# Decoder layer, attention stage: the projections of the next batch spread over all four head steps, the output projection ahead of the transposes

## The chip, the cores and the metric

The kernel runs on one core of a Trainium2 chip. A core has five engines that run on their own and wait for each other through semaphores: TensorE (PE: matmuls and transposes, results into PSUM; its weight loads are listed apart as PEld), VectorE (DVE), ScalarE (ACT), GpSimd (POOL) and SyncE (SP, which here only issues DMAs). PSUM has eight banks of 128 x 512 fp32. The metric is the device time of one execution in microseconds (us).

## The reference

A decoder layer on x of 4 batches x 512 positions x 512 features: x plus attention of its layer norm, then a small cross attention, then a mixture of experts. The change touches the attention alone:

```
q = rope((x @ Wq.T).reshape(B, L, 32, 64))
k = rope((x @ Wk.T).reshape(B, L, 8, 64))
v = (x @ Wv.T).reshape(B, L, 8, 64)
attn = where(causal, q @ k.T * 64 ** -0.5, -inf)      # 4 query heads share a k/v head
out  = (softmax(attn) @ v) @ Wo.T
```

## The kernel before

The attention is worked in 8 groups (one k/v head and its 4 query heads), each group over 4 batches, each batch over 4 heads: 128 **head steps**. The functions `pe_group`, `act_group`, `dve_group` and `pool_group` write out, for each engine, one group's 16 head steps in a fixed order; nothing else sets the order. The first and the last group are written out; the six between run in a hardware loop `Fori` of two passes with three groups in its body (L634, L667, L709, L738; SP's at L607). In a step, c = 4b + h, b being the batch and h the head in it (0 to 3; this text says first to fourth step). Three heads are in work at once: scores and softmax of head n+1, the transposes of the probabilities of head n-1, and PV of head n-2.

All products are made in fp32r from a high and a low part ("hi" is a rounded copy made by ACT, "lo" the rest, made by DVE or POOL), so a projection is 12 matmuls (4 chunks of the features x 3 combinations). One step's parts, by function and line of before:

- `pe_scores` (L197): 8 matmuls into S_BANK. `dve_masked` (L411, at L421) scales and masks them into `probs` and takes the row's extreme; `act_exp` (L307) follows, `dve_recip` (L426), and POOL's `pool_norm` (L540) multiplies with it.
- `pe_ptrans` (L211, at L217): ten 128 x 128 transposes of `probs` in three units: unit 0 (four, T_BANK[0]), unit 1 (four, T_BANK[1]), unit 2 (two, T_BANK[0] again, issued at the start of the next step). `act_pt` makes pt_hi from the bank (L349), `dve_pt` pt_lo (L464, at L409). Unit 0 of the next head waits until unit 2's pt_lo is made, since they share a bank.
- `pe_pv` (L221, at L234): 8 matmuls; `act_opart` (L356) copies one half of the result, `dve_oadd` (L469, at L474) adds the other half into `o_f`. After two heads `act_o` makes o_hi and `dve_o` o_lo.
- `pe_wo` (L237, at L246): output projection of 128 positions, 6 matmuls into WO_BANK, one per step, for the batch before. `dve_woacc` (L480, at L484) adds it to `x_res`. The group's weights for it are split in batch 1: hi by `act_w2` at the end of the second step, lo by `dve_w2` in the third step, where `pe_wo` first waits for them (w2_lo_done).
- `pe_proj` (L179, at L184): one projection of the **next** batch into PJ_BANK. Index r = 2 is k and v together, r = 0 and 1 two heads of q each. `dve_rope_in` (L430) reads the bank, `pool_rope` (L533) and `act_rope` (L315) go on; `dve_q_lo` (L442) makes q's low part for two heads.
- `pe_vt` (L189, at L194): four small transposes of v into PJ_BANK, then `act_v` and `dve_v` read them.

In before, the first three steps of a batch hold one whole projection each (k/v, q of heads 0 and 1, q of heads 2 and 3), the fourth v's transposes. The first output tile of a batch is projected in the third step.

## Time and profile before

| | us |
|---|---|
| timed runs | 1640.63, 1640.20, 1631.22 (median 1640.2) |
| the profiled execution: its own time | 1635.06 |
| its span, first to last instruction | 1633.3 |
| PE busy | 1483.1 (91%) |
| DVE busy | 1372.1 (84%) |
| ACT busy | 1057.7 (65%) |
| POOL busy | 849.6 (52%) |

How to read it: the busy shares are averages over three stages. The layer norms and the first projections take about the first 55 us, the attention groups last until about 1050 us, the rest is cross attention and experts, which the change leaves alone. In a timeline a row is a start, a length, the engine, the line and operation, what it writes and reads, and in brackets the idle time before it and what ended that. Matmuls overlap, so the cost of one is the distance between starts and not its length.

### The profile page before, as it was taken

The page shows a single profiled execution, that of the slowest core. Times are in us where ns is not written, and L with a number is a line of the kernel's source. Part 1 is how long each engine was busy: PE and PEld are TensorE (multiplying, and loading weights), DVE is VectorE, ACT ScalarE, POOL GpSimd, SP SyncE. Part 2 cuts the span into 40 slices and gives each one's busy share as a digit, 9 for nine tenths or more (in the row PEclk, how much of TensorE's full clock was granted, in tenths as well). Part 3 has the DMA queues.
Part 4 walks back from the last instruction along what each step waited for, and adds up shares of the span by engine and source line. Part 5 has one row for each costly group of instructions (what it writes and reads, how often), then busy time and mean ns, then how long its engine had stood idle before and what let it go on. Part 6 is the DMA issues. An engine that isn't in the chain of part 4 may idle for free. (4 is left out here: it accounts for less than half of the span.)

```text
span 1633.3 us, 31312 instructions
## 1 busy us (share of the span) xinstructions
PE 1483.1 (91%) x8951; PEld 1306.6 (80%) x8951; DVE 1372.1 (84%) x3565; ACT 1057.7 (65%) x2464; POOL 849.6 (52%) x1033
## 2 busy tenths in 40 slices
PE   5789999999999899999999999688599999999994
PEld 4678888888888788878878877577489999999993
DVE  7789888898898788988988988577579988998892
ACT  3677777777777677777777777332166666666661
POOL 6667657657657557657657655267612233222321
PEclk9899999999999999999999999967599999999997
DMA  4000000000000000000000000112468778887765
GB/s 175 1 14 20 1 14 21 1 14 21 1 14 20 3 14 21 2 14 21 1 14 1 1 1 1 41 65 92 164 184 243 226 217 220 240 228 219 198 172 135
DMA packets 62032, 124.97 MB, mean 77 GB/s; under 512 B 20942, under 2 KB 21070, under 8 KB 61792
## 3 DMA queue, kind: packets, MB, share of 16 engines
q1 hardware_dynamic: 51408, 102.24, 19.6%
q0 software_dynamic: 10304, 20.59, 6.6%
q8 instruction: 77, 1.26, 0.3%
q14 instruction: 99, 0.81, 0.2%
q10 hardware_dynamic: 144, 0.07, 0.0%
HBM read 106.08 MB, written 24.71 MB: 80 GB/s over the span
## 5 line engine op out<-in xcount | busy, mean ns | idle before, releaser
L312 ACT ACTIVATE probs<-probs,neg_max 128x512 f32<-128x512 f32 (+3 forms) x512 | 281.7, 552 | 46.5 <-DVE neg_max L421 44.2
L545 POOL TENSOR_SCALAR probs<-probs,row_inv 128x512 f32<-128x512 f32 (+3 forms) x512 | 264.3, 535 | 44.4 <-DVE row_inv L428 44.4
L536 POOL TENSOR_TENSOR rot<-rot,sin 128x512 f32<-128x512 f32 (+1 forms) x96 | 123.6, 1288 | 303.4 <-DVE rot L440 299.1
L217 PE MATMUL bank<-ident,probs 128*128 128x128 f32 x1280 | 184.5, 275 | 59.6 <-DVE pt_lo L409 50.1
L409 DVE TENSOR_TENSOR pt_lo<-bank,pt_hi 128x512 fp32r<-128x512 f32 (+1 forms) x384 | 216.3, 591 | 25.8 <-ACT pt_hi L305 25.7
L305 ACT ACTIVATE pt_hi<-bank 128x512 fp32r<-128x512 f32 (+1 forms) x384 | 186.3, 518 | 71.6 <-PE bank L217 63.6
L421 DVE CUSTOM_DVE_ANT_0 probs<-bank,causal 128x512 f32<-128x512 f32 (+3 forms) x512 | 219.7, 482 | 10.1 <-issue 3.6
L1221 POOL DMA_INDIRECT acc<-ctx_raw,idx x46 | 74.5, 1619 | 294.9 <-ACT ctx_raw L1374 280.8
L217 PEld LDWEIGHTS bank<-ident,probs 128*128 128x128 f32 x1280 | 149.9, 140 | 94.9 <-DVE pt_lo L409 54.9
L1302 PE MATMUL bank<-xt_hi,gu_hi 128*128 128x256 f32 x736 | 208.4, 283 | 2.0 <-DVE xt_lo L409 1.5
L1302 PE MATMUL bank<-xt_lo,gu_hi 128*128 128x256 f32 x736 | 206.7, 281 | 0.0
L1302 PE MATMUL bank<-xt_hi,gu_lo 128*128 128x256 f32 x736 | 206.5, 281 | 0.0
L207 PE MATMUL bank<-k_hi,q_st 128*128 128x256 f32 (+2 forms) x512 | 172.3, 347 | 3.2 <-DVE xn_lo L409 3.2
L234 PE MATMUL bank<-pt_hi,v_st 128*128 128x256 f32 (+2 forms) x512 | 171.4, 346 | 1.6 <-DVE pt_lo L409 1.6
L207 PE MATMUL bank<-k_lo,q_st 128*128 128x256 f32 (+2 forms) x512 | 156.9, 328 | 0.0
L234 PE MATMUL bank<-pt_lo,v_st 128*128 128x256 f32 (+2 forms) x512 | 155.8, 326 | 0.0
L184 PE MATMUL bank<-xn_hi,w_hi 128*128 128x512 f32 x384 | 153.2, 399 | 0.4 <-DVE rot L440 0.4
L184 PE MATMUL bank<-xn_lo,w_hi 128*128 128x512 f32 x384 | 151.9, 396 | 0.0
L184 PE MATMUL bank<-xn_hi,w_lo 128*128 128x512 f32 x384 | 151.5, 395 | 0.0
L1302 PEld LDWEIGHTS bank<-xt_hi,gu_hi 128*128 128x128 f32 x736 | 139.2, 189 | 6.2 <-issue 2.8
L1302 PEld LDWEIGHTS bank<-xt_lo,gu_hi 128*128 128x128 f32 x736 | 139.5, 189 | 2.8
L1302 PEld LDWEIGHTS bank<-xt_hi,gu_lo 128*128 128x128 f32 x736 | 139.1, 189 | 0.0
(196 smaller groups left out, 3912.8 us busy)
## 6 DMA issues: line engine op xcount, KB each, us to landing
gu_raw<-in_gate_up SPq DMA_DIRECT2D x92, 512.0 KB, 4.2
dn_raw<-in_down SPq DMA_DIRECT2D x92, 256.0 KB, 3.8
w_raw<-in_wqkv SPq DMA_DIRECT2D x8, 768.0 KB, 4.1
w_raw<-in_wo_rows SPq DMA_DIRECT2D x8, 512.0 KB, 3.5
h_rows<-ln_h SPq DMA_DIRECT2D x16, 256.0 KB, 2.0
acc<-x_res SPq DMA_DIRECT2D x4, 1024.0 KB, 4.7
x_res<-in_x SPq DMA_DIRECT2D x3, 1024.0 KB, 11.4
ctx_raw<-in_ctx SPq DMA_DIRECT2D x2, 512.0 KB, 6.7
```

Of the source, the lines that this page charges most:

```text
L184: last = nc.tensor.matmul(PJ_BANK[:, :], w1[sp][:, c, r * P:(r + 1) * P], xn[mp][:, c, b * L:(b + 1) * L], start=first, stop=(c == DC - 1 ...
L207: last = nc.tensor.matmul(S_BANK[k][:, at:at + cols], q_st[:, h, i * P:(i + 1) * P], kk[:, kb, 0:cols], start=(a == 0), stop=(a == 1))
L217: last = nc.tensor.transpose(T_BANK[u % 2][:, k * P:(k + 1) * P], probs[:, hb, P_AT[i] + j * P:P_AT[i] + (j + 1) * P], ident[:, :])
L234: last = nc.tensor.matmul(dst, v_st[:, vb, j, :], rhs, start=(j == 0 and a == 0), stop=(j == QB - 1 and a == 1))
L305: nc.scalar.activation(dst, src, ACT.Copy).then_inc(sem_, 1)
L312: nc.scalar.activation(row, row, ACT.Exp, bias=neg_max[:, hb, i:i + 1], scale=-1.0, accum_out=row_sum[:, hb, i:i + 1]).then_inc(s["exp_don ...
L409: nc.vector.tensor_tensor(dst, src, hi.bitcast(F32), ALU.subtract).then_inc(sem_, 1)
L421: nc.vector.tensor_tensor_reduce(out=probs[:, hb, P_AT[i]:P_AT[i] + (i + 1) * P], in0=S_BANK[k][:, at:at + (i + 1) * P], in1=causal[:, (QB ...
L536: nc.gpsimd.tensor_tensor(rot[0:rows, :], rot[0:rows, :], sin[0:rows, :], ALU.mult).then_inc(s["rot_sin"], 1)
L545: nc.gpsimd.tensor_scalar(row, row, row_inv[:, hb, i:i + 1], 0.0, ALU.mult, ALU.add).then_inc(s["pnorm_done"], 1)
L1221: nc.gpsimd.indirect_dma_start(out=acc, out_offset=bass.IndirectOffsetOnAxis(ap=idx[:, 2 * tau + h:2 * tau + h + 1], axis=0), in_=y[:, 2 * ...
L1302: last = nc.tensor.matmul(GU_BANK[u % 3][:, side * TILE:(side + 1) * TILE], gu[sp_][:, ib, c, side, :], xts[mp][:, k, c, :], start=first, ...
```

## The change

- The twelve matmuls of a projection are cut into two pieces in different steps, and each of the four steps gets nine: the fourth step the first 9 of k/v (for the batch after the next), the first step the other 3 and, behind PV, the first 6 of q for heads 0 and 1, the second step the other 6 and, behind PV, the first 3 of q for heads 2 and 3, the third step the other 9.
- v's transposes stand at the fourth step's start and write T_BANK[1] in place of PJ_BANK, so they wait for the second pt_lo of the head before; the transposes of unit 1 wait for v_lo in that step.
- The output projection stands ahead of the eight transposes in every step (before: only in the first step). On DVE, adding it to x_res stands ahead of o_f.
- ACT's and DVE's work on the second pair of q heads moves from the next batch's first step to the fourth step; v's from the fourth step's end to its start.
- The group loops are written out on all engines, SP among them.

```
+KV_FIRST, Q01_FIRST, Q23_FIRST = 9, 6, 3
...
+        def pe_proj(pe, b, r, begin=0, end=3 * DC):
+            for n in range(begin, end):
+                c, (sp, mp) = n // 3, PASSES[n % 3]
+                last = nc.tensor.matmul(PJ_BANK[:, :], w1[sp][:, c, r * P:(r + 1) * P], xn[mp][:, c, b * L:(b + 1) * L],
+                                        start=(n == 0), stop=(n == 3 * DC - 1))
+            if end == 3 * DC:
+                last.then_inc(s["proj_done"], 1)
...
+        def pe_vt(pe, m, heads_before):
             pe.wait_ge(s["vt_done"], m + 1)
             settled(pe)
+            wait(pe, s["pt_lo_done"], heads_before and 3 * heads_before - 1)
             for j in range(QB):
-                last = nc.tensor.transpose(PJ_BANK[:, j * HD:(j + 1) * HD], v_t[:, j * P:(j + 1) * P], ident[HD:P, HD:P])
+                last = nc.tensor.transpose(T_BANK[1][:, j * HD:(j + 1) * HD], v_t[:, j * P:(j + 1) * P], ident[HD:P, HD:P])
...
+            if u == 1 and n % G == 2 and n < HEADS * GROUPS - G:
+                pe.wait_ge(s["v_lo_done"], n // G + 2)
...
                 if d_begun:
                     pe_ptrans(pe, dn_ - 1, (r + d - 1) % 3, 2)
+                if h == 3 and next_batch:
+                    pe_vt(pe, m + 1, dn_)
                 if more:
                     pe_scores(pe, n + 1, m if h < G - 1 else m + 1, (h + 1) % G, (b + (h == G - 1)) % 2)
...
                 if h == 0 and next_batch:
-                    pe.wait_ge(s["v_lo_done"], m + 1)
-                    pe_proj(pe, (b + 1) % B, 2)
+                    pe_proj(pe, (b + 1) % B, 2, KV_FIRST)
                 if h == 1 and next_batch:
...
+                    pe_proj(pe, (b + 1) % B, 0, Q01_FIRST)
                 if h == 2 and next_batch:
...
+                    pe_proj(pe, (b + 1) % B, 1, Q23_FIRST)
+                if h == 3 and batch_after:
+                    if b == 2:
+                        pe.wait_ge(s["w1_lo_done"], 3 * g + 4)
                     pe.wait_ge(s["rope_in"], 3 * m + 6)
-                    pe_vt(pe, m + 1)
+                    pe_proj(pe, (b + 2) % B, 2, 0, KV_FIRST)
                 if dh == 3 and d_last:
                     pe_wo(pe, dm - 1, (db - 1) % 2, 2)
-                if d_here:
-                    pe_ptrans(pe, dn_, (r + d) % 3, 0)
-                    pe_ptrans(pe, dn_, (r + d) % 3, 1)
-                if d_begun:
-                    pe_pv(pe, dn_ - 1, dm if dh else dm - 1, (d + 1) % 2, (db if dh else db + 1) % 2)
                 if dh in (1, 2) and d_last:
                     if dh == 1 and db == 1:
                         pe.wait_ge(s["w2_lo_done"], 2 * g + 2)
                     pe_wo(pe, dm - 1, (db - 1) % 2, dh - 1)
                 if dh == 0 and d_before_last:
                     pe_wo(pe, dm - 2, db % 2, 3)
+                if d_here:
+                    pe_ptrans(pe, dn_, (r + d) % 3, 0)
+                    pe_ptrans(pe, dn_, (r + d) % 3, 1)
+                if d_begun:
+                    pe_pv(pe, dn_ - 1, dm if dh else dm - 1, (d + 1) % 2, (db if dh else db + 1) % 2)
+                if h == 0 and next_batch:
...
+                    pe.wait_ge(s["rope_in"], 3 * m + 4)
+                    pe.wait_ge(s["vt_done"], m + 2)
+                    pe_proj(pe, (b + 1) % B, 0, 0, Q01_FIRST)
+                if h == 1 and next_batch:
...
+                    pe.wait_ge(s["rope_in"], 3 * m + 5)
+                    pe_proj(pe, (b + 1) % B, 1, 0, Q23_FIRST)
...
-                if h == 0 and begun and front:
-                    act_rope(act, m, 2, b % 2)
-                if h in (1, 2) and next_batch:
+                if h == 3 and next_batch:
+                    act_v(act, m + 1, (b + 1) % 2)
+                if h and next_batch:
                     act_rope(act, m + 1, h - 1, (b + 1) % 2)
...
-                if h == 0 and begun and front:
-                    dve_q_lo(dve, m, 2, b % 2)
-                if h == 2 and next_batch:
-                    dve_q_lo(dve, m + 1, 1, (b + 1) % 2)
+                if h == 3 and next_batch:
+                    dve_v(dve, m + 1, (b + 1) % 2)
+                if h >= 2 and next_batch:
+                    dve_q_lo(dve, m + 1, h - 1, (b + 1) % 2)
...
-                with pe.Fori(0, (GROUPS - 2) // 3) as q:
-                    for i in range(1, 4):
-                        pe_group(pe, 3 * q + i, i % 3)
+                for g in range(1, GROUPS - 1):
+                    pe_group(pe, g, g % 3)
```

PE, third step of batch 1 in the last group: `w_hi`/`w_lo` with `o_hi`/`o_lo` is the output projection, `probs` the transposes, `v_st` PV. Before, from the second unit of transposes:

```order
L217 MATMUL bank<-ident,probs 128x128 [waits pt_lo_done]
L217 MATMUL bank<-ident,probs 128x128 x3
L234 MATMUL bank<-pt_hi,v_st 128x512 [waits oadd_done,v_lo_done,pt_lo_done]
L234 MATMUL bank<-pt_lo,v_st 128x512
L234 MATMUL bank<-pt_hi,v_st 128x384
L234 MATMUL bank<-pt_lo,v_st 128x384
L234 MATMUL bank<-pt_hi,v_st 128x256
L234 MATMUL bank<-pt_lo,v_st 128x256
L234 MATMUL bank<-pt_hi,v_st 128x256
L234 MATMUL bank<-pt_lo,v_st 128x256
L246 MATMUL bank<-w_hi,o_hi 128x512 [waits wo_out_done,o_lo_done,w2_lo_done]
L246 MATMUL bank<-w_lo,o_hi 128x512
```

Of the change, at the same place, from the last two projection matmuls (`xn`):

```order
L186 MATMUL bank<-xn_lo,w_hi 128x512
L186 MATMUL bank<-xn_hi,w_lo 128x512
L251 MATMUL bank<-w_hi,o_hi 128x512 [waits wo_out_done,o_lo_done,w2_lo_done]
L251 MATMUL bank<-w_lo,o_hi 128x512
L251 MATMUL bank<-w_hi,o_lo 128x512
L251 MATMUL bank<-w_hi,o_hi 128x512
L251 MATMUL bank<-w_lo,o_hi 128x512
L251 MATMUL bank<-w_hi,o_lo 128x512
L222 MATMUL bank<-ident,probs 128x128 [waits pt_lo_done,pnorm_done]
L222 MATMUL bank<-ident,probs 128x128 x3
```

The output projection with its wait for w2_lo_done has moved from behind PV to ahead of the transposes.

PE, fourth step that follows it: the last two matmuls of the scores (`k_lo`, `k_hi`), v's transposes (`v_and_o`), the eight transposes of the probabilities. Before:

```order
L207 MATMUL bank<-k_hi,q_st 128x256
L207 MATMUL bank<-k_lo,q_st 128x256
L194 MATMUL bank<-ident,v_and_o 128x64 [waits rope_in,vt_done]
L194 MATMUL bank<-ident,v_and_o 128x64 x3
L217 MATMUL bank<-ident,probs 128x128 [waits pt_lo_done,pnorm_done]
L217 MATMUL bank<-ident,probs 128x128 x3
```

Of the change, from the start of that step:

```order
L222 MATMUL bank<-ident,probs 128x128 [waits pt_lo_done]
L222 MATMUL bank<-ident,probs 128x128
L197 MATMUL bank<-ident,v_and_o 128x64 [waits vt_done,pt_lo_done]
L197 MATMUL bank<-ident,v_and_o 128x64 x3
L210 MATMUL bank<-k_hi,q_st 128x512 [waits masked_done,q_lo_done,k_lo_done]
```

v's transposes now stand ahead of the scores and wait for a pt_lo; between the scores and the eight transposes stand nine projection matmuls and the output projection (rows like those shown above).

DVE, the same fourth step in the first group, from pt_lo of unit 2 on: `q_st` is q's low part, `x_res` the sum with the output projection, `o_f` the sum of PV's halves. Before:

```order
L409 TENSOR_TENSOR pt_lo<-bank,pt_hi 128x256 [waits pt_hi_done]
L428 RECIPROCAL row_inv<-row_sum 128x4 [waits exp_done]
L409 TENSOR_TENSOR pt_lo<-bank,pt_hi 128x512 [waits pt_hi_done] x2
L409 TENSOR_TENSOR v_st<-bank,v_st 128x4x64 [waits v_hi_done]
L474 TENSOR_TENSOR o_f<-bank,v_and_o 64x512 [waits o_lo_done,opart_done]
L484 TENSOR_TENSOR x_res<-bank,x_res 128x512 [waits wo_done]
```

Of the change:

```order
L422 TENSOR_TENSOR pt_lo<-bank,pt_hi 128x256 [waits pt_hi_done]
L422 TENSOR_TENSOR v_st<-bank,v_st 128x4x64 [waits v_hi_done]
L459 TENSOR_TENSOR q_st<-rope,q_st 64x512 [waits rope_hi]
L460 TENSOR_TENSOR q_st<-rope,q_st 64x512
L441 RECIPROCAL row_inv<-row_sum 128x4 [waits exp_done]
L422 TENSOR_TENSOR pt_lo<-bank,pt_hi 128x512 [waits pt_hi_done] x2
L497 TENSOR_TENSOR x_res<-bank,x_res 128x512 [waits wo_done]
L487 TENSOR_TENSOR o_f<-bank,v_and_o 64x512 [waits o_lo_done,opart_done]
```

v's low part and two instructions for q now stand ahead of the reciprocal and of the two pt_lo; o_f stands last.

## Rows read from the trace of the kernel before

**Rows 1.** Windows: busy us (and instructions) of each engine in one group.
```profile
319.58:442.60 123.02, 117.18 (x674) 101.44 (x673) 109.89 (x291) 94.08 (x237) 78.15 (x100) 1.00 0.04 12
```

**Rows 2.** Waits in the attention: engine, who ended them, us, times, longest.
```profile
PE bank L217 <- DVE pt_lo L409: 46.2, 47, 2.6
```

**Rows 3.** Timeline of PE: a second step, then the third step's start and output projection.
```profile
332.56 0.38 PE L217 MATMUL bank<-ident,probs 128*128 128x128 f32 x2
...
334.08 0.40 PE L184 MATMUL bank<-xn_hi,w_hi 128*128 128x512 f32 x1
...
336.82 1.03 PE L217 MATMUL bank<-ident,probs 128*128 128x128 f32 x8
337.61 0.48 PE L234 MATMUL bank<-pt_hi,v_st 128*128 128x512 f32 x1
...
338.99 0.40 PE L246 MATMUL bank<-w_hi,o_hi 128*128 128x512 f32 x1
...
340.38 0.38 PE L217 MATMUL bank<-ident,probs 128*128 128x128 f32 x2
...
347.04 0.50 PE L246 MATMUL bank<-w_hi,o_hi 128*128 128x512 f32 x1
```

**Rows 4.** Timeline of PE: v's transposes in a fourth step and what follows.
```profile
319.58 0.46 PE L194 MATMUL bank<-ident,v_and_o 64*128 64x64 f32 x4
321.19 1.09 PE L217 MATMUL bank<-ident,probs 128*128 128x128 f32 x8 [1.15 <-DVE pt_lo L409]
```

**Rows 5.** Timeline of PE: v's transposes, first and last of 31 such rows.
```profile
74.28 0.46 PE L194 MATMUL bank<-ident,v_and_o 64*128 64x64 f32 x4
...
1001.95 0.46 PE L194 MATMUL bank<-ident,v_and_o 64*128 64x64 f32 x4
```

**Rows 6.** Waits in the attention that nothing in the profile explains: ACT.
```profile
ACT pt_hi L305 <- issue: 5.1, 1, 5.1
```

**Rows 7.** Timeline of ACT and DVE behind the PV of rows 3.
```profile
339.19 0.59 ACT L305 ACTIVATE v_and_o<-bank 64x512 f32<-64x512 f32 x1 [0.51 <-PE bank L234]
...
339.82 0.68 DVE L474 TENSOR_TENSOR o_f<-bank,v_and_o 64x512 f32<-64x512 f32 x1 [0.21 <-ACT v_and_o L305]
340.58 0.69 DVE L484 TENSOR_TENSOR x_res<-bank,x_res 128x512 f32<-128x512 f32 x1
```

**Rows 8.** Timeline of DVE: the third step of batch 1, masking to pt_lo.
```profile
341.37 0.69 DVE L421 CUSTOM_DVE_ANT_0 probs<-bank,causal 128x512 f32<-128x512 f32 x1
...
343.02 0.42 DVE L409 TENSOR_TENSOR pt_lo<-bank,pt_hi 128x256 fp32r<-128x256 f32 x1
343.36 0.80 DVE L409 TENSOR_TENSOR o_lo<-o_f,o_hi 128x512 fp32r<-128x512 f32 x1
...
345.61 1.29 DVE L409 TENSOR_TENSOR w_lo<-w_raw,w_hi 128x512 fp32r<-128x512 f32 x2
...
348.13 1.26 DVE L409 TENSOR_TENSOR pt_lo<-bank,pt_hi 128x512 fp32r<-128x512 f32 x2
```

**Rows 9.** Timeline of ACT at the same place.
```profile
340.53 0.63 ACT L305 ACTIVATE o_hi<-o_f 128x512 fp32r<-128x512 f32 x1 [0.75 <-DVE o_f L474]
341.07 1.14 ACT L305 ACTIVATE w_hi<-w_raw 128x512 fp32r<-128x512 f32 x2
342.24 0.39 ACT L305 ACTIVATE pt_hi<-bank 128x256 fp32r<-128x256 f32 x1
```

**Rows 10.** Windows as in rows 1; behind POOL stands the granted clock.
```profile
1018.00:1021.00 3.00, 3.00 (x12) 2.71 (x12) 1.41 (x3) 1.09 (x3) 2.05 (x4) 0.50 0.00 0
...
135.00:137.70 2.70, 0.99 (x9) 0.72 (x7) 2.59 (x11) 1.45 (x5) 2.70 (x5) 1.00 0.00 0
```

**Rows 11.** Timeline of PE: a step of the last batch.
```profile
1017.00 1.41 PE L217 MATMUL bank<-ident,probs 128*128 128x128 f32 x8 [2.13 <-DVE pt_lo L409]
```

**Rows 12.** Timeline of DVE in a first step, and of POOL beside rows 8.
```profile
327.77 0.68 DVE L409 TENSOR_TENSOR o_lo<-o_f,o_hi 128x512 fp32r<-128x512 f32 x1
...
341.57 2.06 POOL L545 TENSOR_SCALAR probs<-probs,row_inv 128x512 f32<-128x512 f32 x4
```

More of the change, by code:

```diff
@@ L177, in pe_ln @@
             last.then_inc(s["lnt_done"], 1)
-        def pe_proj(pe, b, r):
-            first = True
-            for c in range(DC):
-                for sp, mp in PASSES:
-                    last = nc.tensor.matmul(PJ_BANK[:, :], w1[sp][:, c, r * P:(r + 1) * P], xn[mp][:, c, b * L:(b + 1) * L],
-                                            start=first, stop=(c == DC - 1 and (sp, mp) == PASSES[-1]))
-                    first = False
-            last.then_inc(s["proj_done"], 1)
-        def pe_vt(pe, m):
+        def pe_proj(pe, b, r, begin=0, end=3 * DC):
[6 more added lines that the diff above has]
+        def pe_vt(pe, m, heads_before):
             pe.wait_ge(s["vt_done"], m + 1)
             settled(pe)
+            wait(pe, s["pt_lo_done"], heads_before and 3 * heads_before - 1)
             for j in range(QB):
-                last = nc.tensor.transpose(PJ_BANK[:, j * HD:(j + 1) * HD], v_t[:, j * P:(j + 1) * P], ident[HD:P, HD:P])
+                last = nc.tensor.transpose(T_BANK[1][:, j * HD:(j + 1) * HD], v_t[:, j * P:(j + 1) * P], ident[HD:P, HD:P])
             last.then_inc(s["v_tr"], 1)
@@ L395, in act_group @@
                     act_pt(act, dn_, d % 2, 1)
-                if h == 3 and next_batch:
-                    act_v(act, m + 1, (b + 1) % 2)
                 if d_begun:
@@ L522, in dve_group @@
                     dve_woacc(dve, dm - 1, (db - 1) % B, 2)
-                if h == 3 and next_batch:
-                    dve_v(dve, m + 1, (b + 1) % 2)
-                if d_begun:
-                    dve_oadd(dve, dn_ - 1, (d - 1) % 2, HEADS // 2 * g + (d - 1) // 2)
                 if dh in (1, 2) and d_last:
@@ L606, in _ @@
                 sp_w2(sp, 0)
-                with sp.Fori(1, GROUPS) as g:
+                for g in range(1, GROUPS):
                     sp_w1(sp, g)
@@ L666, in _ @@
                 act_group(act, 0, 0)
-                with act.Fori(0, (GROUPS - 2) // 3) as q:
-                    for i in range(1, 4):
-                        act_group(act, 3 * q + i, i % 3)
+                for g in range(1, GROUPS - 1):
+                    act_group(act, g, g % 3)
                 act_group(act, GROUPS - 1, (GROUPS - 1) % 3)
@@ L708, in _ @@
                 dve_group(dve, 0, 0)
-                with dve.Fori(0, (GROUPS - 2) // 3) as q:
-                    for i in range(1, 4):
-                        dve_group(dve, 3 * q + i, i % 3)
+                for g in range(1, GROUPS - 1):
+                    dve_group(dve, g, g % 3)
                 dve_group(dve, GROUPS - 1, (GROUPS - 1) % 3)
@@ L737, in _ @@
                 pool_group(pool, 0, 0)
-                with pool.Fori(0, (GROUPS - 2) // 3) as q:
-                    for i in range(1, 4):
-                        pool_group(pool, 3 * q + i, i % 3)
+                for g in range(1, GROUPS - 1):
+                    pool_group(pool, g, g % 3)
                 pool_group(pool, GROUPS - 1, (GROUPS - 1) % 3)
```

22 lines of the change are left out of this document (11 added, 11 removed).

## The prediction

> **What bounds the kernel now.** The page comes first: one execution spans 1633.3 us, 1635.1 with what lies around it; the sum below is made against that. The three timed runs have a median of 1640.2, 0.3% above it, and spread by 0.6%, so about 1% is what a comparison of this kernel can tell from no change. Then the busy time by stretch. One group of attention (four batches, sixteen head steps) takes 123.02 us, of which TensorE (PE) works 117.18, VectorE (DVE) 109.89, ScalarE (ACT) 94.08, GpSimd (POOL) 78.15 [rows 1]. PE is the bound, DVE is close behind. The table of waits then says what PE waits for: pt_lo, 46.2 us in 47 waits [rows 2]. The timeline of PE says where. In a batch's second step there is no idle time: transposes of unit 2 and scores 1.52 us, twelve projection matmuls 2.74 (0.228 each), eight transposes 0.79, PV 1.38, output projection 1.39, together 7.82 [rows 3]. In the fourth step only v's four transposes (0.46) stand behind the scores, and PE idles 1.15 us until pt_lo is there [rows 4].
>
> From the first v transposes of the group loop to the last, 31 rows, 927.67 us go by [rows 5]: 30 batches, among them one loop end, where ACT stood still for 5.1 us with nothing to wait for [rows 6]. Without it a batch takes 30.76 (123.02/4). PE's own work in it is 3 x 7.82 + 7.82 - 2.74 + 0.46 = 29.0. So some 1.76 us a batch, 7.0 a group, are waits; that is all the change can win there.
>
> **Balance of the projections.** No matmul is removed. Each step now has nine: steps one to three 7.82 - 3 x 0.228 = 7.14, the fourth 7.14 + 0.46 = 7.60, together 29.0, as before. The old wait of 1.15 is gone in the fourth step, since nine matmuls and the output projection (3.44) stand between scores and transposes, and DVE needs only about 2 (below). What is late next?
>
> DVE ends a step with x_res and then o_f. ACT's copy of PV starts 1.58 after PV's first matmul, o_f 0.63 later, and the next instruction that has to wait for nothing else 0.8 after that [rows 3, 7]: together 3.0, of which PV itself covers 1.38. Today the output projection runs behind PV and covers the rest. After the change masking starts some 1.6 us into the next step where PV was last (into steps one and four), and about 0.85 us into step three, since three projection matmuls (0.68) run behind PV in step two. I count from a step's start S.
> - Third step. DVE needs 1.99 from the start of masking to o_lo and 0.80 for that [rows 8]: done at S + 3.64. PE wants o_lo for the output projection at S + 1.52 + 2.05 = S + 3.57. Wait 0.1.
> - Fourth step. In rows 8, masking to the end of the two pt_lo is 349.39 - 341.37 = 8.02, less 1.21 for the w_lo pair: 6.81, so S + 7.66 of the third step, whose PE work ends at 7.24. v's transposes now write a T bank and need the second pt_lo: 0.49 late, less 0.13 for two transposes in front. Wait 0.36.
> - First step. Between scores and transposes stand 0.68 + 1.39, so PE wants the transposes at S + 3.59. Masking from 1.5 to 1.6, 1.65 long, and pt_lo, 0.42 [rows 8], give 3.6 to 3.7. Wait 0 to 0.1; I count 0.
>
> The second step has 1.37 + 1.39 in front and waits for nothing. So a plain batch is 29.0 + 0.46 = 29.46. Bounds: 29.0 (no wait) and 29.9 (each twice as long).
>
> Hidden moves, with their cover. v in the fourth step: DVE has read the bank by S + 4.1 (1.6, masking 1.65, pt_lo 0.42, and as much again for v), PE comes to unit 1 at about S + 5.8 (7.6 - 1.38 - 0.4): 1.7 spare. q_lo of the second pair, moved there: its rope input is made in the third step by S + 6.4 (0.85 + 348.13 - 341.37 - 1.21 [rows 8]), and DVE comes to q_lo 4.8 us later, with two POOL instructions and one ACT pair between. The k/v projection begun in the fourth step needs the same rope input, also there before it. POOL's own order is unchanged. SP's two weight DMAs per group keep their semaphores and come a group ahead. If any of these covers is gone it costs what it is late by, 31 times.
>
> **The output projection in front.** Its first tile of a group's batch one needs the group's new weights, split hi on ACT at the end of step two and lo on DVE in step three. This is the added wait. Now: step three starts at 340.38, w_lo starts at 345.61 and takes 1.29, and the projection, behind PV, starts at 347.04, hardly late [rows 3, 8]. After: PE is there at S + 3.57. ACT's chain is o_hi, w_hi, pt_hi [rows 9]; with o_f at the end of step two instead of before x_res, o_hi starts at S + 0.95, w_hi ends at 2.7, pt_hi at 3.1, so DVE's pt_lo follows at 3.1, o_lo at 3.5, and from o_lo to the end of w_lo it is 346.90 - 343.36 = 3.54 [rows 8]: near 7.0. PE stands 3.4 us. Queued behind it are eight transposes and PV; ACT's pt_hi and DVE's last pt_lo, x_res and o_f wait for those. Bounds: 2.8 (DVE as in rows 8 from S + 0.85: 6.38) to 3.9.
>
> Does the pause cost clock? Before 1017.00 PE idled 2.13 us, and 1018 to 1021 then ran at 0.50 of full clock, the 1.2 GHz level; where it worked 0.99 us in 2.70, at 135 us, the clock stayed at 1.00 [rows 10, 11]. A pause of 3.4 lies beyond both. 3.0 us at half clock are 1.5 lost, no fall is 0; I take 1.4. With PE slowed, v's wait of 0.36 goes. Net 3.4 + 1.4 - 0.4 = 4.4, in all 8 groups: 35.2.
>
> In batch two ACT also splits w1 (0.57 each): pt_hi and masking's followers slip, 0.6 per group, 7 groups: 4.2.
>
> **Loops written out.** The 5.1 us at the loop's end go [rows 6]. What straight code costs is bounded by 0 and by one such pause a group (7 x 5.1, with which the sum would be some 1664; that goes with rivals 2 and 4). I take 0: the loop's body is three groups of straight code today, and the pause occurs once in all [rows 6].
>
> **Last group.** Steps without projections: before the transposes at 1017.00 PE idled 2.13 [rows 11], and 1.39 of output projection now stands there. I take 2.5 gained over the four steps (bounds 0 and 4).
>
> **Sum.** 30 x 29.46 + 35.2 + 4.2 = 923.2, against 927.67: 4.5 less; with 2.5, 7.0 less. 1635.1 - 7.0 = **1628**. The balance wins 1.3 per batch (39 us) and the loop 5, the weight wait eats 35 of it.
>
> **A rule of the skill.** DVE's o_lo took 0.68 us with POOL idle (327.77) and 0.80 while POOL normalised (343.36) [rows 8, 12]. So a collision costs 0.12, and in the new third step it is already in the 0.8. The Trainium skill, SBUF — State Buffer, section on two separate sides, says that such a pair is an exclusive lock held for the whole instruction, the loser fully blocked. By the row the sum stays; by the page it is the third rival below.
>
> **The rivals.**
> 1. The weight wait is cheaper: the clock stays up and the steady waits halve. For it: the trace has a fall and a pause without one [rows 10, 11], and the 0.46 is a sum of small lags. Against it: the pause expected is longer than either. 8 x 1.4 + 30 x 0.23 = 18 less: 1610.
> 2. Slower: the first step's cover is too thin. It decides when masking starts later than S + 1.5 there; DVE's 27.5 us a batch (109.89/4) in 29.5 leave little to catch up with. If o_f comes 1.0 later, PE waits 1.0 in every first step, as it did for the same pt_lo in the fourth: 31 us more, 1659. Against it: the first step loses q_lo's two instructions (1.4 us [rows 8]) on DVE.
> 3. The port blocks. o_lo in the third step meets the last 0.3 us of POOL's normalisation; the delay goes to PE's wait and to v's: 30 x 0.3 = 9 more, 1637.
> 4. The change doesn't do what it says: PE's waits move to other places and stay at 1.76 a batch, with the weight wait on top: 30 x 30.76 + 39.4 - 927.67 = 34.5 more, less 2.5: 1667. Against it: 3.44 us of cover in front of a wait that was 1.15.
>
> **How the numbers follow.** Forecast 0.47, rival 1 0.33, rival 2 0.05, rival 3 0.11, rival 4 0.04. Faster by over 1% needs under about 1619 against this execution (1624 by the median): rival 1 and a little of the forecast, 0.36. Slower by over 1% is 1651 and more: rivals 2 and 4, 0.09. Same 0.55. The range takes in rival 1 down to 1605 and rival 3 with the long weight wait (8 x 0.5) up to 1645, as the median lies above the profiled run. The forecast alone: 1618 to 1637.
>
> **What would show it.** In the changed profile: fourth steps without a wait before the eight transposes; waits of 0.3 to 0.5 before v's transposes; eight waits of 3 us or more of the output projection for w_lo, each followed by a stretch near half clock; no pause of ACT near 541. Wrong would be weight waits under 2 us, or new waits of the first step's transposes.

## The result, and the profile after

The changed kernel takes 1649.1 us (median of 5 runs, 1646.7 to 1651.2), the kernel before 1635.7 (1631.2 to 1640.6) beside it: a ratio of 1.0085, with a 95% interval of 1.0061 to 1.0109. It is slower by just under 1%, inside the 1% that the forecast took for no change, with the interval reaching just past it. The forecast was 1628 and its range ended at 1645; both are missed.

Below are the waits of the changed kernel's attention (engine, who ended them, us, times, longest), the lines that answer to [rows 2]. The wait of 46.2 us for pt_lo has shrunk to 16.8, but a wait for the new weights has come, eight times, and one for o_lo. ACT's pause at a loop end [rows 6] is not in the list any more.

```profile
PE bank L251 <- DVE w_lo L422: 27.0, 8, 3.5
PE bank L222 <- DVE pt_lo L422: 16.8, 43, 1.6
PE bank L251 <- DVE o_lo L422: 5.8, 9, 2.8
```

The first and the last row of v's transposes, as [rows 5]:

```profile
72.47 0.46 PE L197 MATMUL bank<-ident,v_and_o 64*128 64x64 f32 x4 [0.16 <-DVE pt_lo L422]
...
1013.14 0.46 PE L197 MATMUL bank<-ident,v_and_o 64*128 64x64 f32 x4
```

A window over one group, as [rows 1] (length, then the busy time of PE, PEld, DVE, ACT and POOL with the instructions, then the granted clock, DMA share and GB/s):

```profile
322.92:448.81 125.89, 120.15 (x672) 102.25 (x672) 111.73 (x291) 95.20 (x238) 78.69 (x100) 0.99 0.04 12
```

From first to last 940.67 us go by instead of 927.67, and a group takes 125.89 instead of 123.02. The span is 1644.9, so all that lies outside these 30 batches is 704.2 us, against 705.6 before: the loss sits in the attention alone.

Where in a group? The distances between v's transposes, as means over the groups, with the number of them, are worked out from the 31 rows of either trace ("plain" is the batch that ends in batch 0's fourth step; no weights are split in it):

| batch | before | forecast | changed |
|---|---|---|---|
| plain (7) | 30.20, once 35.86 at the loop end | 29.46 | 29.96 (four of 29.85 to 29.87, three of 30.07 or 30.08) |
| 1, with the wait for the output weights (8) | 30.89 | 33.86 | 34.20 (33.20 to 34.73) |
| 2, with GpSimd's share of the projection weights (8) | 31.14 | 30.06 in 7 | 30.80 |
| 3 (7) | 30.61 | 29.46 | 30.14 |

Three places carry this. First the weights, in PE's timeline (start, length, engine, line, operation; in brackets the idle time before it and who ended it):

```profile
344.92 0.38 PE L222 MATMUL bank<-ident,probs 128*128 128x128 f32 x2
...
352.01 0.50 PE L251 MATMUL bank<-w_hi,o_hi 128*128 128x512 f32 x1 [3.37 <-DVE w_lo L422]
...
357.30 0.38 PE L222 MATMUL bank<-ident,probs 128*128 128x128 f32 x2
```

The third step of batch 1 begins at 344.92, PE stands 3.37 us for w_lo, and the step lasts 12.38 instead of 7.4. What PE does right after this pause runs at the lower of its two clock levels, 1.2 GHz, as a window of the same trace shows (0.50, the last but two). It does so behind six of the eight such pauses; behind the other two, of 3.37 and 3.35 us, the clock stays at 1.00, as in the second window, and these batches take 33.20 and 33.24 us instead of 34.7:

```profile
352.80:356.20 3.40, 3.40 (x13) 2.92 (x12) 0.79 (x3) 0.70 (x2) 2.83 (x3) 0.50 0.51 158
...
604.40:607.80 3.40, 3.33 (x23) 2.83 (x22) 1.89 (x5) 1.43 (x3) 2.83 (x3) 1.00 0.48 154
```

Second, a first step, in the timelines of PE and, behind them, of DVE:

```profile
328.92 0.48 PE L239 MATMUL bank<-pt_hi,v_st 128*128 128x512 f32 x1
...
330.29 0.38 PE L222 MATMUL bank<-ident,probs 128*128 128x128 f32 x2
...
333.64 0.39 PE L251 MATMUL bank<-w_hi,o_lo 128*128 128x512 f32 x1
334.24 1.06 PE L222 MATMUL bank<-ident,probs 128*128 128x128 f32 x8 [0.21 <-DVE pt_lo L422]
...
329.39 1.29 DVE L422 TENSOR_TENSOR pt_lo<-bank,pt_hi 128x512 fp32r<-128x512 f32 x2 [1.18 <-ACT pt_hi L320]
330.60 0.68 DVE L497 TENSOR_TENSOR x_res<-bank,x_res 128x512 f32<-128x512 f32 x1
331.31 0.69 DVE L487 TENSOR_TENSOR o_f<-bank,v_and_o 64x512 f32<-64x512 f32 x1
332.03 0.69 DVE L434 CUSTOM_DVE_ANT_0 probs<-bank,causal 128x512 f32<-128x512 f32 x1
...
333.68 0.42 DVE L422 TENSOR_TENSOR pt_lo<-bank,pt_hi 128x256 fp32r<-128x256 f32 x1
```

The step starts at S = 330.29. DVE still has x_res and o_f to do, and masks from 332.03, S + 1.74; unit 2's pt_lo starts 1.65 later. PE has issued its last matmul at 333.64 and could go on 0.23 later, at 333.87; it goes on at 334.24. That is 0.37 us of wait in a step that the forecast let wait for nothing (the 0.21 in brackets counts only from the end of the last matmul's length). Third, the step before and the step after, which were foreseen: the output projection of a third step starts at 318.82, 0.20 late behind the last projection matmul (318.39), and v's transposes stand 0.46 behind the step's start at 322.46, of which two transposes need 0.13:

```profile
318.39 0.39 PE L186 MATMUL bank<-xn_hi,w_lo 128*128 128x512 f32 x1
318.82 0.50 PE L251 MATMUL bank<-w_hi,o_hi 128*128 128x512 f32 x1
...
322.46 0.38 PE L222 MATMUL bank<-ident,probs 128*128 128x128 f32 x2
322.92 0.46 PE L197 MATMUL bank<-ident,v_and_o 64*128 64x64 f32 x4
```

### The profile page after: what moved, and what is told of

It is laid out like the page before. It is cut to its first block and busy times, and to the rows that moved or that the text cites. A ratio compares the mean times of both kernels' runs of the same rounds, so it can differ in the third digit from the quotient of the medians.

```text
span 1644.9 us, 28746 instructions
## 1 busy us (share of the span) xinstructions
PE 1500.1 (91%) x8951; PEld 1305.9 (79%) x8951; DVE 1383.5 (84%) x3565; ACT 1065.4 (65%) x2464; POOL 858.3 (52%) x1033
## 5 line engine op out<-in xcount | busy, mean ns | idle before, releaser
L556 POOL TENSOR_SCALAR probs<-probs,row_inv 128x512 f32<-128x512 f32 (+3 forms) x512 | 273.1, 554 | 100.7 <-DVE row_inv L441 100.7
L222 PEld LDWEIGHTS bank<-ident,probs 128*128 128x128 f32 x1280 | 153.6, 143 | 54.4 <-issue 24.2
```

The costliest lines, as they stand in the source:

```text
L222: last = nc.tensor.transpose(T_BANK[u % 2][:, k * P:(k + 1) * P], probs[:, hb, P_AT[i] + j * P:P_AT[i] + (j + 1) * P], ident[:, :])
L556: nc.gpsimd.tensor_scalar(row, row, row_inv[:, hb, i:i + 1], 0.0, ALU.mult, ALU.add).then_inc(s["pnorm_done"], 1)
```

## The experiments

The theory W at the outset was the forecast's: the balance and the written-out loops win, the wait for the weights eats it. The rival L was that DVE is late everywhere once nothing runs behind PV. (The letters of theories and rivals are new in each experiment.)

**1. The first tile behind PV again.** From the changed kernel, in batch 1's third step alone:

```
-                if dh in (1, 2) and d_last:
-                    if dh == 1 and db == 1:
-                        pe.wait_ge(s["w2_lo_done"], 2 * g + 2)
+                if dh in (1, 2) and d_last and not (dh == 1 and db == 1):
...
+                if dh == 1 and db == 1 and d_last:
+                    pe.wait_ge(s["w2_lo_done"], 2 * g + 2)
+                    pe_wo(pe, dm - 1, (db - 1) % 2, dh - 1)
```

The second place is behind PV; on DVE the addition to x_res moves behind o_f in the same way.

> The changed kernel, but in the third step of a group's batch 1 alone the output projection stands behind PV again (and x_res behind o_f on DVE), as before the change; all other steps keep it in front. Theory W (the weights of the output projection come too late for its new place): in the trace of the changed kernel the interval between v's transposes is 34.7 us for batch 1 (33.2 where the clock stays up) and 29.9 to 30.1 for batch 0. Behind PV the projection comes 2.2 us later than in front, so most of the 3.4 us wait goes and the clock does not fall: about 4 of the 4.6 us per group, 8 groups: 1649 - 32 = 1617, that is faster than the kernel before by 1.1%. Rival L (VectorE is late everywhere, the weight wait only gives it time to catch up): the time comes back as other waits in the steps that follow, and at most half is won: 1633.

Measured: 1626.4 us (6 runs), 0.9939 of before (0.9921 to 0.9958). The weights cost 22.7 us against the changed kernel, which lies between the theories. The wait for w_lo did not vanish, it is a third. Waits, then PE's timeline and a window at one of these places:

```profile
PE bank L251 <- DVE w_lo L423: 8.2, 8, 1.2
PE bank L251 <- DVE o_lo L423: 7.8, 17, 2.8
```

```profile
344.29 0.50 PE L251 MATMUL bank<-w_hi,o_hi 128*128 128x512 f32 x1 [1.01 <-DVE w_lo L423]
```

```profile
344.30:347.70 3.40, 3.00 (x14) 2.04 (x15) 3.40 (x8) 1.83 (x4) 2.04 (x2) 1.00 0.49 154
```

After a pause of 1.01 us the clock stays at 1.00, here and behind the other seven (1.00 to 1.15 us), so no fall is to be paid. Batch 1 takes 31.28 us instead of 34.20. The plain batch stays, at 30.07; something else is wrong too.

**2. The balance alone.** The output projection behind PV in steps two to four, as before, and x_res behind o_f; all else as changed (the projections in pieces, v's place, no loops).

> The changed kernel with the output projection behind PV in steps two to four, and x_res behind o_f, as before the change: the pieces of the projections, v's place and the written-out loops alone. Theory W: the weight wait goes (32 us), and since the output projection runs behind PV while VectorE finishes o_f, masking starts about 1 us into a step instead of 1.0 to 1.7, so the waits of the first step (0.36) and of o_lo in the third (0.2) go too, 31 x 0.55 = 17: 1649 - 49 = 1600. Rival T (nine matmuls alone are too little cover, the output projection is needed in front): the second step has only 1.37 us between scores and transposes and the fourth 2.05; each then waits 0.3 to 0.8, up to 1 us a batch: 1649 - 32 - 17 + 31 = 1631.

Measured: 1610.0 us (4 runs), 0.9855 (0.9829 to 0.9881): faster than either kernel. A plain batch takes 29.69. The time lies between the two expectations. What W counted on has gone: in a plain batch the first step takes 7.11 us and the third 7.14, PE's work alone. But the second takes 7.45 and the fourth 8.00, 0.3 and 0.4 above PE's work, the least that T gave them. So the order in front, weights or not, costs 39 us, 16 more than experiment 1 gave back (12.2 of these 16 from first to last v: 906.28 us against 918.52).

**3. The loops alone**, written out in the kernel before, nothing else.

> The kernel before with its group loops written out on all engines and nothing else. Theory W: the one loop end goes, where ScalarE stood 5.1 us and the batch took 35.86 instead of 30.58: 5.3 us less, 1630.4, nothing lost elsewhere. Rival: straight code costs instruction fetches, up to what the changed kernel is slower than forecast (21 us): 1636 to 1657.

Measured: 1636.0 us (12 runs), 0.9999 (0.9981 to 1.0016). The batch with 35.86 us is gone from the trace (30.24 there), and the time has not followed. In its trace from first to last v it is 925.90 us, 1.8 less than before, though the loop end gave back 5.6: two other batches have a stretch at the lower clock in them and are 1.6 us longer than their like (32.78 and 32.33 instead of 31.2 and 30.8). A pair of equal pauses shows that this comes and goes (PE's rows, and a window behind each):

```profile
107.18 1.94 PE L217 MATMUL bank<-ident,probs 128*128 128x128 f32 x8 [1.74 <-POOL probs L545]
...
139.96 1.06 PE L217 MATMUL bank<-ident,probs 128*128 128x128 f32 x8 [1.74 <-POOL probs L545]
```

```profile
107.20:110.40 3.20, 3.20 (x12) 3.01 (x13) 1.49 (x4) 2.25 (x7) 2.24 (x5) 0.50 0.00 0
140.00:142.70 2.70, 2.70 (x19) 2.52 (x20) 1.59 (x4) 2.35 (x8) 2.70 (x5) 1.00 0.00 0
```

The same 1.74 us, once with 0.50 behind it and once with 1.00. Whether the loops are worth nothing or their gain is spent in this way in most executions, this run leaves open.

**4. The order in front alone**: the kernel before with the output projection ahead of the transposes in every step and x_res ahead of o_f; whole projections, loops kept.

> The kernel before with the output projection in front of the eight transposes in every step and x_res ahead of o_f, and nothing else (whole projections, loops as before). Theory W: the fourth step's wait shrinks from 1.66 (1.15 of it idle by the profile) to about 0.4, 30 x 1.2 = 36 less; the weight wait appears, 2.7 us since twelve matmuls stand in front, plus 1.5 where the clock falls, 8 x 3.5 = 28 more: 1636 - 8 = 1628. Rival L: masking starts 1.6 us into every step, the fourth step keeps a wait of 1 us or more: 1636 - 15 + 28 = 1649, as slow as the whole change.

Measured: 1686.0 us (4 runs), 1.0315 (1.0289 to 1.034). Both expectations fell, by more than 35 us. In the trace batch 1 takes 35.30 us instead of 30.89, which is 35 us over 8 groups, and the other batches are longer by 0.1 to 0.5. Its waits, and a row of PE's timeline at a second step's start:

```profile
PE bank L217 <- DVE pt_lo L409: 32.0, 34, 1.6
PE bank L246 <- DVE w_lo L409: 27.4, 8, 3.5
```

```profile
376.61 0.44 PE L217 MATMUL bank<-ident,probs 128*128 128x128 f32 x2 [0.74 <-DVE pt_lo L409]
```

The old wait for pt_lo, 1.15 in the fourth step [rows 4], is not there; in its place stands one of 0.74 at the start of the second step (376.61). Cover in one step made DVE late in another. That is not lag "everywhere", and it asked for a test of where the cover lies.

**5. A thicker first step.** The changed kernel, with two of the k/v products moved from the fourth step to the first, ahead of its transposes:

```
-KV_FIRST, Q01_FIRST, Q23_FIRST = 9, 6, 3
+KV_FIRST, Q01_FIRST, Q23_FIRST = 7, 6, 3
```

> The changed kernel with 7 instead of 9 of a batch's k and v products in the fourth step: 5 instead of 3 stand ahead of the transposes of the first step, 0.30 us more cover there (2 products at 0.15 to 0.23 us), as much less in the fourth. Theory T (thin cover: VectorE is late at the first step by 0.2 to 0.5 us, and the step's own cover sets what of that is seen): the first step's wait goes and none comes in the fourth, 31 times 0.2 to 0.36 us, 1638 to 1643. Rival L (VectorE is the slower engine over the whole step circle, so that cover given to one step is taken from the next): the plain batch stays at 29.96 us within 0.1, 1646 to 1652.

Measured: 1636.8 us (10 runs), 1.0008 (0.999 to 1.0025), 12 us less than the changed kernel; a plain batch takes 29.61 instead of 29.96. Theory T holds, with a time just below its range: the first step was covered too thinly. It now takes 7.58 us with two products more, 7.52 before, so the wait of 0.37 is gone; the fourth, 7.82 before, takes 7.37 and had cover to spare.

**6. Shorter additions on DVE.** Experiment 1 with

```
-            tile = x_res[:, b * QB + t, :]
-            nc.vector.tensor_tensor(tile, src[:, :], tile, ALU.add).then_inc(s["wo_out_done"], 1)
+            cols = D if m >= B * GROUPS - 1 else 64
+            tile = x_res[:, b * QB + t, 0:cols]
+            nc.vector.tensor_tensor(tile, src[:, 0:cols], tile, ALU.add).then_inc(s["wo_out_done"], 1)
```

> The kernel with the first tile behind (the first of these experiments), with the residual addition of each output tile cut to its first 64 of 512 columns in all but the last batch, so that a part of the output projection is left out of the result and VectorE has about 0.5 us less to do in each step; TensorE does the same work. It is read by the intervals between v's transposes alone, since what follows attention gets other data. Theory L (VectorE's lag is what the output projection in front costs): the plain batch falls from 30.07 us to 29.7 or below, and the 15 us of waits for o_lo at the output projection fall to under 8. Rival R (the waits come from ScalarE's and TensorE's order, PV to o_part to o_f to o_hi): the plain batch stays within 0.1 us of 30.07.

Measured, in one run: the plain batch falls from 30.07 to 29.64, the waits for pt_lo from 17.5 to 11.6 us and those for o_lo from 7.8 to 4.0 by the table of waits (the 15 us of the expectation were not counted by that table and don't compare). These are its lines:

```profile
PE bank L222 <- DVE pt_lo L423: 11.6, 23, 1.1
PE bank L251 <- DVE o_lo L423: 4.0, 2, 2.6
```

Rival R falls and theory L holds: x_res in DVE's queue ahead of o_f and the masking is a part of what PE waits for. It is not all of it in the first step, which falls from 7.52 to 7.33 us where PE's work is 7.14. There o_f now waits for ACT's copy (PE, then DVE):

```profile
320.78 0.38 PE L222 MATMUL bank<-ident,probs 128*128 128x128 f32 x2
...
321.60 0.68 DVE L488 TENSOR_TENSOR o_f<-bank,v_and_o 64x512 f32<-64x512 f32 x1 [0.31 <-ACT v_and_o L321]
322.32 0.69 DVE L435 CUSTOM_DVE_ANT_0 probs<-bank,causal 128x512 f32<-128x512 f32 x1
```

Masking starts at S + 1.54, 0.20 earlier than in the changed kernel, and the transposes at 324.53, S + 3.75, still 0.18 later than PE could. So in the first step x_res makes about half of the wait, and the chain from PV over ACT's copy and o_f the other half. The third step (7.63 to about 7.35) gives the rest of the 0.43.

**7. The balance with loops.** Experiment 2 with the hardware loops of before.

> The kernel of the balance alone (1610 us), with the loops over the middle six groups kept as in the kernel before instead of written out. Theory W (a loop end costs about 5 us, as the trace of before shows it once): 1615 us. Rival S (the loops are worth nothing in time, as the run with the loops alone had it): 1608 to 1612 us.

Measured: 1615.2 us (4 runs), 0.9863 (0.9833 to 0.9893). That is 5.2 above experiment 2, where W puts it, but the kernel before, run beside each, differed too (1634.6 here, 1637.2 there): the two ratios are 0.0008 apart, 1.3 us, and their intervals overlap. So the time doesn't decide between W and S. The traces do for the loop end: from first to last v 909.65 us go by, 3.4 more than in experiment 2, and the extra length is in one place, a plain batch with 33.67 us at the loop's end where the other six take 29.70 to 29.74, and there PE stood with nothing that the profile shows to wait for:

```profile
535.04 0.43 PE L221 MATMUL bank<-ident,probs 128*128 128x128 f32 x2 [2.02 <-issue]
```

So a loop end costs about 4 us in the trace; that writing the loops out wins as much in the time is not shown.

**8. The fourth step in front alone.** Experiment 2, with the output projection ahead of the transposes and x_res ahead of o_f in the fourth step only.

> The kernel of the balance alone (1610 us), with the output projection in front of the transposes, and the residual addition ahead of o_f, in the fourth step alone (the first has both in either kernel). Theory O (it is the third step, where the output projection meets an o_lo that VectorE has just begun, that costs the 16 us between the first two experiments): 1604 to 1611 us. Rival D (each step in which nothing runs behind PV costs alike, VectorE being late at the next one's start): 1614 to 1620 us.

Measured: 1632.9 us (10 runs), 0.9973 (0.9954 to 0.9993), 23 above experiment 2, and 19.3 from first to last v (925.53 against 906.28). Theory O falls. D named the kind of loss and not its size: by either count one step's order costs more than what lies between experiments 1 and 2 (16 and 12.2). The trace shows the first step of the changed kernel again (PE, then DVE; of the eight transposes, here and in the next rows, the window shows the first ones):

```profile
296.73 0.38 PE L222 MATMUL bank<-ident,probs 128*128 128x128 f32 x2
300.67 0.85 PE L222 MATMUL bank<-ident,probs 128*128 128x128 f32 x6 [0.22 <-DVE pt_lo L424]
...
298.46 0.69 DVE L436 CUSTOM_DVE_ANT_0 probs<-bank,causal 128x512 f32<-128x512 f32 x1
```

Masking starts at S + 1.73, the transposes at S + 3.94 (changed: 1.74 and 3.95). In experiment 2, where the output projection ran behind PV in the fourth step, the first step's masking starts at 292.24, S + 0.98, and nothing waits:

```profile
291.26 0.38 PE L222 MATMUL bank<-ident,probs 128*128 128x128 f32 x2
294.83 0.38 PE L222 MATMUL bank<-ident,probs 128*128 128x128 f32 x2
...
292.24 0.69 DVE L434 CUSTOM_DVE_ANT_0 probs<-bank,causal 128x512 f32<-128x512 f32 x1
```

It is the step **after** the one in front that pays. In the changed kernel the second and third steps were in front too, which gives the second step cover against its own lag; with the fourth step alone the second takes 7.56 us, 0.11 more than in experiment 2, and waits 0.26 as well.

**9. Both mends**: experiment 1 and experiment 5 together.

> The two mends together: the changed kernel with the first tile of the output projection behind PV in batch 1's third step, and with 7 instead of 9 of a batch's k and v products in the fourth step. Theory C (what the output projection in front costs is the wait for the weights and a first step that is covered too thinly, and nothing else): the mends add up, 1649 - 23 - 12 = 1614 us, plain batch 29.6 us, within 4 us of the kernel of the balance alone (1610). Rival F (the order in front costs in itself, by o_lo in the third step): the wait for o_lo of the first of these experiments, 15 us, stays and the time stays above 1618 us.

Measured: 1612.1 us (4 runs), 0.9844 (0.9816 to 0.9871), plain batch 29.60. Theory C holds in its sum: the mends alone were worth 22.7 and 12.4 us, 35.1 together, and 37.0 are measured, within 2 us of the balance alone, with the order in front still there in all other steps (against the kernel before beside each, experiments 2 and 9 are 0.9855 and 0.9844). Its "nothing else" does not hold. The rival's wait for o_lo stays (6.8 us in the table, of which 2.8 are one wait of the last batch), and by starts the third step of a plain batch takes 7.56 us where PE's work is 7.14. The order in front pays for that in the second step, 7.11 us here and 7.45 in experiment 2.

**10. and 11. Going on from the balance alone**: one product of q moved from behind the first step's PV to the second step (`Q01_FIRST` 6 to 5), and then v's transposes behind the fourth step's scores.

> The kernel of the balance alone (1610 us) with 5 instead of 6 of the products of q's first pair behind PV in the first step, and so 7 instead of 6 ahead of the transposes of the second step, which wait 0.15 us for pt_lo in every batch of its trace. Theory T (cover at the place of the wait): 31 times 0.15 us, 1604 to 1607 us. Rival L (VectorE's lag moves with it): 1609 to 1612 us.

> The kernel of the run before it (5 of 6 products behind PV in the first step), and in the fourth step v's transposes behind the scores instead of ahead of them, where they wait 0.16 us for pt_lo in every batch. Theory T: that wait goes, another 31 times 0.16 us, 1599 to 1602 us. Rival A (ScalarE takes v's halves 1.4 us later, its exponentials stand behind them in its order, and the transposes of the fourth step or of the first wait instead): 1607 us or more.

Measured: 1604.9 us (4 runs), 0.98 (0.9773 to 0.9827), for the first, as T said: the fastest of all, 2% below the kernel before. By batches it is not as even as T has it: the plain batch falls from 29.69 to 29.46 and batch 1 from 30.88 to 30.66, but batch 3 stays at 29.70, its second step 0.23 longer, which is what rival L said of all. Its group, beside [rows 1] and the changed one:

```profile
312.82:433.11 120.29, 117.87 (x672) 100.50 (x672) 110.95 (x291) 94.54 (x238) 77.62 (x100) 1.00 0.04 12
```

PE works 117.87 of 120.29 us, so by busy time 2.4 us a group are left to win by order; by the distances between matmul starts (29.0 a batch) it is 4.3. The second gave 1607.2 (4 runs), 0.9816 (0.9786 to 0.9845); from first to last v it takes 901.54 us where the first takes 900.90, and no batch's mean differs by more than 0.1. v's wait is gone and nothing is won by it, so theory T falls: the fourth step of a plain batch is 0.20 us shorter, and the first and second are 0.07 and 0.15 longer. Rival A has the time right; it named the fourth step or the first for the new waits, and most of them are in the second.

Why the second step waits at all is seen in experiment 2, where DVE is not late there (the step starts at S = 298.39; DVE, then PE):

```profile
299.37 0.69 DVE L434 CUSTOM_DVE_ANT_0 probs<-bank,causal 128x512 f32<-128x512 f32 x1 [0.35 <-PE bank L210]
...
301.58 1.06 PE L222 MATMUL bank<-ident,probs 128*128 128x128 f32 x8
```

DVE has to wait for the scores, masks from S + 0.98, and the transposes come at S + 3.19 all the same. What stands ahead of the transposes has to last 3.2 us even when DVE has caught up; with six products it lasts 2.89, with seven 3.12.

**12. GpSimd's split cut short**, for batch 2, whose extra length the forecast had put on ACT. The changed kernel with

```
-            vec.tensor_tensor(w1[1][:, :, r * P:(r + 1) * P], w1_raw[:, :, r * P:(r + 1) * P],
-                              w1[0][:, :, r * P:(r + 1) * P].bitcast(F32), ALU.subtract).then_inc(s["w1_lo_done"], 1)
+            cols = DC if g == 0 else 1
+            vec.tensor_tensor(w1[1][:, 0:cols, r * P:(r + 1) * P], w1_raw[:, 0:cols, r * P:(r + 1) * P],
+                              w1[0][:, 0:cols, r * P:(r + 1) * P].bitcast(F32), ALU.subtract).then_inc(s["w1_lo_done"], 1)
```

> The changed kernel with GpSimd's subtraction for the lo part of the new projection weights, three in a group of batches, cut to 128 of its 512 columns in all groups but the first; the rest of that lo part keeps the old group's numbers, and what follows attention gets other data, so it is read by the intervals between v's transposes. In the changed kernel's trace VectorE's subtraction for q_st takes 1.67 and 1.61 us, instead of 0.69, in the two steps of batch 2 where it meets GpSimd's of 1.74 us. Theory P (the two engines' subtractions keep each other out, and this is what makes batch 2 1.0 us longer than a plain one): q_st there falls to 0.7 to 1.1 us and batch 2's interval from 30.95 to 30.1 to 30.5. Rival S (ScalarE's splits of the weights, 0.6 us each ahead of its pt_hi, make batch 2 long, as the prediction had it): the interval stays at 30.8 or more.

Measured, in one run: batch 2 takes 30.03 to 30.17 us in the seven groups in which the changed kernel has 30.86 to 31.00. Theory P holds, and ACT's splits, which are still there, leave at most the 0.1 to 0.2 us above the plain batch. The changed kernel's rows, then this one's:

```profile
382.95 1.74 POOL L469 TENSOR_TENSOR w_lo<-w_raw,w_hi 128x512 fp32r<-128x512 f32 x1
...
383.56 1.67 DVE L459 TENSOR_TENSOR q_st<-rope,q_st 64x512 fp32r<-64x512 f32 x1
```

```profile
382.09 0.91 POOL L470 TENSOR_TENSOR w_lo<-w_raw,w_hi 128x128 fp32r<-128x128 f32 x1
...
382.71 0.83 DVE L459 TENSOR_TENSOR q_st<-rope,q_st 64x512 fp32r<-64x512 f32 x1
```

DVE's subtraction takes 1.67 us while GpSimd's runs, 0.83 when that one is short; elsewhere mostly 0.69. In both it ends 0.54 us after GpSimd's (384.69 to 385.23, 383.00 to 383.54).

## Why the prediction was wrong

Against the forecast's sum for the attention, 923.2 us, the trace has 940.67: 17.5 too few. By the table of batches:

- **The plain batch: 0.50 a batch, 15.0 us in 30, and 0.37 of it, 11 us, in the step that failed, "First step. ... Wait 0 to 0.1; I count 0."** The mechanism stood there, and again as rival 2 with its point, masking later than S + 1.5; it was given 0.05 and a price of 1.0. Measured are S + 1.74 and 0.37. Two terms were too small. The sum let o_f follow ACT's copy, 2.21 behind PV's first matmul [rows 3, 7]; it comes 2.39 behind it (328.92 to 331.31), since DVE is only then through with the pt_lo pair and x_res, which now stands ahead of o_f. And nothing was counted between the end of pt_lo and PE's next matmul, where the changed trace has 0.14 (333.68 + 0.42 to 334.24). Experiment 6 parts the two: with o_f right behind ACT's copy, as the sum had it, masking comes at S + 1.54, inside the forecast's 1.5 to 1.6, and PE still waits 0.18; x_res ahead of o_f, with masking 0.20 later, adds the rest. A forecast of 3.6 to 3.7 against a need of 3.59 was no zero, and 31 repeats hung on it. What was set against rival 2, that the first step loses q_lo's two instructions on DVE, has no bearing: in the kernel before they stand behind unit 2's pt_lo, which is the end of this wait (and rows 8 don't show them). Experiments 5, 8 and 9 show this wait made, moved and taken away, and it was worth 12 to 14 us in the time.
- **The third step's o_lo**, 0.1 forecast, 0.20 measured in four of the seven plain batches and about 0.4 in three; **the fourth step's v**, 0.36 forecast, 0.33 measured (the sum's own figures, 7.66 less 7.24, give 0.42 late and not 0.49, so 0.29). With the first step 0.90 to 1.1 a batch; the mean is 0.96 above the 29.0 of PE's work.
- **The weights: right.** The pause of 3.4 us was measured as 3.35 to 3.47, the fall of the clock came behind six of the eight, and batch 1 lies 4.24 above the plain one where 4.4 was forecast (1.3 us too much in all). Experiment 1 gives 22.7 us back and not 35, since w_lo still comes 1.0 late behind PV.
- **Batch 2: 0.6 forecast, 0.84 measured in 8** (2.5 us), and for the wrong reason: not ACT's splits but the two engines' subtractions keeping each other out (experiment 12). It was to be read from the trace of before, whose batch 2 is 0.94 longer than its plain one. The Trainium skill, SBUF — State Buffer, section on two separate sides, says that a VectorE instruction with two SBUF inputs and a GpSimd one that reads SBUF take a port pair by turns, the later one fully blocked; the traces agree (0.69 becomes 1.67, 0.83 when GpSimd's takes 0.91).
- **Rival 3, in part right.** It had the two engines collide at o_lo in the third step. In the changed kernel either of them can be the one that is late there. Where o_lo takes 0.68 us and GpSimd's four normalisations 2.61 instead of 2.06, the plain batch takes 29.85 to 29.87 (four of seven); where o_lo takes 0.86 or 0.91, it takes 30.07 or 30.08 (three). The rows of one of each, GpSimd's ahead of DVE's:

```profile
316.39 2.61 POOL L556 TENSOR_SCALAR probs<-probs,row_inv 128x512 f32<-128x512 f32 x4
318.08 0.68 DVE L422 TENSOR_TENSOR o_lo<-o_f,o_hi 128x512 fp32r<-128x512 f32 x1
...
442.05 2.07 POOL L556 TENSOR_SCALAR probs<-probs,row_inv 128x512 f32<-128x512 f32 x4
443.75 0.91 DVE L422 TENSOR_TENSOR o_lo<-o_f,o_hi 128x512 fp32r<-128x512 f32 x1
```

  That is 0.2 us in three plain batches, where the rival had 0.3 in every one; no run takes this collision away, so its price is read from these two kinds of batch alone.
- **Batch 3: 0.18 above the plain one**, 1.3 us in 7, forecast none; its cause stays open.
- **Outside the batches** 1.4 us were won, 2.5 forecast.

**Balance and loops: right in kind.** Without the order in front a plain batch takes 29.69 us (experiment 2), where 29.46 was forecast with it; experiment 10 reaches 29.46 by another split of the waits. A loop end costs about 4 us in the trace of experiment 7 and 5.7 in that of before; in the time neither experiment 3 nor experiment 7 shows it clear of the noise. Rival 1 (cheap weights) fell with the pause of 3.37. Rival 4, waits only moved, is what experiment 4 shows of the order in front when it stands alone.

The outcome within 1% had 0.55, and there it fell, but by another way than those it was given for: 0.05 for a mechanism whose threshold the forecast itself had placed within 0.1 us of its estimate was too little, and so the range ended below the time.

## What to carry to other kernels

A matmul stage moved in front of the one that another engine depends on gives cover in its own step and takes it from the next: whoever reads the last product starts later in that one (here masking at S + 1.74 instead of S + 0.98, for 1.39 us of matmuls moved). Count for every step the start of that engine's work and the cover ahead of its consumer, and where they meet within the error of the spacing, book the wait with a real chance, times its repeats, or add cover there; two products of 0.23 us in the right step were worth more than 12 us. When a weight's last conversion feeds the stage that is moved up, leave that one instance where it was.

## What was not expected of the hardware

- Equal pauses of PE had the lower clock behind them in one case and the full clock in another: of 1.74 us in experiment 3, and of 3.35 to 3.47 us in the changed kernel, where it fell behind six of eight. Behind 1.00 to 1.15 us (experiment 1) it fell in none of eight. A fall shows as 34.7 us against 33.2 in batch 1 of the changed kernel, so about 1.5 us.
- DVE starts the same two instructions, x_res and o_f, 0.71 us apart in one step (330.60, 331.31) and 0.60 in another (307.87, 308.47). It was 0.60 in all 36 steps of the changed kernel in which ACT's copy had ended before x_res began, and 0.7 or more in 61 of the 80 others; why is not shown.
- A VectorE subtraction of two SBUF tensors stretches from 0.69 to about 1.6 to 1.7 us beside a GpSimd one (1.67 beside one of 1.74, 1.61 beside one of 1.32): seven times in the kernel before, fourteen times in the changed one. The second seven fell into the fourth step, which had the cover, and were hardly seen in the time (batch 3: 30.14 us, and 30.07 in experiment 12).
